# The output bias of the slot values: from row-of-ones products on TensorE to an addition on GpSimd

## The reference, cut to what matters

```python
x_in = _ln(ctx, lnkv_g, lnkv_b)              # 16 batches x 77 rows x 128
k = x_in @ wk + bk
v = x_in @ wv + bv
slots = q_mu + exp(q_logsig) * noise         # noise is the normalised x
for _ in range(3):
    prev = slots
    q = _ln(slots, lnq_g, lnq_b) @ wq + bq
    attn = softmax(k @ q.T / scale, over the slots) + 1e-8
    attn = attn / attn.sum(over the 77 rows)
    upd = attn.T @ v
    slots = upd @ wu + bu + prev
    h = _ln(slots, lnm_g, lnm_b) @ w1 + b1
    slots = gelu(h) @ w2 + b2 + slots
    slots = _ln(slots + x_cls, lnp_g, lnp_b)
```

## Time and profile before

| | |
|---|---|
| median of 3 runs | 912.81 us (910.27 to 913.75) |
| the profiled execution | 913.3 us, its span 911.5 us |
| TensorE matmul busy | 781.2 us, 86% |
| VectorE busy | 568.4 us, 62% |
| ScalarE busy | 529.7 us, 58% |
| GpSimd busy | 360.8 us, 40% |
| mean granted TensorE clock | 0.912 of full speed |

### The profile page before, as it was taken

How to read it: one execution, slowest core, us unless ns; L and a number is a source line. 1 busy time by engine, 2 the same in 40 slices (tenths; PEclk the granted TensorE clock), 3 DMA queues, 4 the chain that set the end, 5 groups by cost and what they waited for, 6 DMA issues and landing times.

```text
span 911.5 us, 18113 instructions
## 1 busy us (share of the span) xinstructions
PE 781.2 (86%) x5705; PEld 645.1 (71%) x5705; DVE 568.4 (62%) x1974; ACT 529.7 (58%) x1144; POOL 360.8 (40%) x561
## 2 busy tenths in 40 slices
PE   6988799999999999989988778999968786861693
PEld 5766678878888788777876547999646565651693
DVE  1667777787776667776767653333658787874012
ACT  3665566667666677656756422333359898841462
POOL 1233444343443333332346562665413232226363
PEclk9999899999999999999989979999757979785797
DMA  8324405340701520301140044886600000001574
GB/s 263 111 66 148 143 1 168 113 178 25 267 1 30 177 57 5 99 1 33 57 161 26 25 145 135 246 248 191 215 0 1 1 1 1 1 1 39 166 200 137
DMA packets 82057, 88.54 MB, mean 97 GB/s; under 512 B 6156, under 2 KB 69852, under 8 KB 81324
## 3 DMA queue, kind: packets, MB, share of 16 engines
q1 hardware_dynamic: 78475, 80.19, 29.1%
q0 software_dynamic: 3488, 7.20, 2.2%
HBM read 69.03 MB, written 35.17 MB: 114 GB/s over the span
## 4 chain that ended last, share of the span: by engine, by line
PE 58%; DVE 20%; issue 8%; ACT 6%; POOL 5%; DMA 1%; DVEq 0%; SPq 0%; POOLq 0%; ACTq 0%
PE bank L706 6%; PE bank L1017 6%; PE bank L700 6%; DVE sb_smax L1531 4%; PE bank L733 4%; PE bank L773 3%; DVE sb_row_sum L1540 3%; PE bank L742 3%; PE bank L1025 3%; PE bank L838 3%; PE bank L758 2%; PE bank L1126 2%; PE bank L1134 2%; PE bank L715 2%; DVE sb_st_all L1857 2%
## 5 line engine op out<-in xcount | busy, mean ns | idle before, releaser
L2035 POOL TENSOR_TENSOR sb_expd<-sb_expd,sb_rden 128x512 f32<-128x512 f32 (+1 forms) x128 | 112.4, 879 | 243.5 <-DVE sb_rden L1544 243.3
L1531 DVE TENSOR_REDUCE sb_smax<-bank 128x4 f32<-128x512 f32 (+1 forms) x128 | 74.0, 578 | 66.7 <-PE bank L733 35.6
L2127 POOL TENSOR_TENSOR sb_rstd_all<-sb_rsq_all,sb_halves 128x4 f32<-128x4 f32 x44 | 45.2, 1028 | 131.6 <-DVE sb_rsq_all L1864 131.6
L1254 ACT ACTIVATE sb_expd<-sb_shifted 128x512 f32<-128x512 f32 (+1 forms) x128 | 69.7, 544 | 43.4 <-DVE sb_shifted L1534 42.4
L1540 DVE TENSOR_REDUCE sb_row_sum<-sb_expd 128x4 f32<-128x512 f32 (+1 forms) x128 | 73.0, 570 | 8.4 <-ACT sb_expd L1254 8.4
L1534 DVE TENSOR_TENSOR sb_shifted<-bank,sb_smax 128x512 f32<-128x512 f32 (+1 forms) x128 | 74.9, 585 | 4.4
L700 PE MATMUL bank<-sb_h1T,sb_watt 128*128 128x128 f32 x512 | 71.3, 291 | 4.2 <-ACT sb_h1T L1153 2.3
L700 PEld LDWEIGHTS bank<-sb_h1T,sb_watt 128*128 128x128 f32 x512 | 65.5, 204 | 6.8 <-DMA sb_watt<-att_w 2.7
L1017 PE MATMUL bank<-sb_blk_xT,sb_up_w 128*128 128x128 f32 x456 | 57.1, 275 | 0.0
L1017 PEld LDWEIGHTS bank<-sb_blk_xT,sb_up_w 128*128 128x128 f32 x456 | 54.0, 192 | 0.0
L1824 DVE TENSOR_TENSOR sb_hid<-bank,sb_hid 128x384 f32<-128x384 f32 x38 | 21.2, 558 | 51.1 <-ACT sb_hid L1302 51.1
(11 more groups left out here) (270 smaller groups left out, 2006.9 us busy)
## 6 DMA issues: line engine op xcount, KB each, us to landing
sb_up_w<-gate_up SPq DMA_DIRECT2D x38, 384.0 KB
sb_v<-v_all SPq DMA_DIRECT2D x16, 576.0 KB, 6.6
rows_b<-pad_b SPq DMA_DIRECT2D x7, 1105.0 KB, 9.8
rows_a<-pad_a SPq DMA_DIRECT2D x7, 975.0 KB, 8.0
sb_up_w<-w1b SPq DMA_DIRECT2D x23, 256.0 KB
v_all<-sb_moe_w SPq DMA_DIRECT2D x14, 308.0 KB
sb_blk_x<-rows_a SPq DMA_DIRECT2D x38, 65.0 KB, 3.3
sb_picked<-back_a SPq DMA_DIRECT2D x4, 512.0 KB, 5.5
```

Of the source, the lines that this page charges most:

```text
L1254: act.activation(exp_of(i, s, j), shifted[:, u % 2, :, 0:n], ACT.Exp, scale=DH ** -0.5).then_inc(exp_done, 1)
L1531: dve.tensor_reduce(smax[:, u % 2, :], s_in, X, ALU.max).then_inc(max_done, 1)
L2035: pool.tensor_tensor(e, e, rden[:, u % 2, :].unsqueeze(2).broadcast_to([P, QH, n]), ALU.mult).then_inc(norm_done, 1)
```

## The change

The 16 row-of-ones products (32 MATMUL records) leave TensorE. `vu` is stored without the bias, and GpSimd adds it in place afterwards, with one TENSOR_TENSOR of 77 x 512 for each group, a new step "bias_u" in the order table. By the table's numbers GpSimd's order becomes: root_o(-1, 0), bias_u 0, bias_u 1, root_q(0, 0), root_o(-1, 1), root_q(0, 1), bias_u 2, root_o(-1, 2), root_q(0, 2), bias_u 3, root_m(0, 0). TensorE waits for `vu_ready` ahead of each of its 12 updates, besides the wait that it had.

```diff
 SLOT_STEPS = {
     (-1,): {
         "add": (-7.7126, -8.1139, -3.1663, -2.2100),
+        "bias_u": (-10.493, -11.492, -11.4, -11.7),
     },
...
+        vu_ready = sem("sl_vu_ready")
...
                 for n in range(4):
-                    pe.matmul(t[0:C, n * D:(n + 1) * D], ones[0:1, 0:C], R["bu"][0:1, :], start=True, stop=False)
-                    mm = pe.matmul(t[0:C, n * D:(n + 1) * D], vT[:, 4 * g + n, :], wus, start=False, stop=True)
+                    mm = pe.matmul(t[0:C, n * D:(n + 1) * D], vT[:, 4 * g + n, :], wus, start=True, stop=True)
                 mm.then_inc(pre_slot_full, 1)
...
                 if step == "update":
                     pe.wait_ge(att_ready, nth("shares", it, g))
+                    pe.wait_ge(vu_ready, nth("bias_u", -1, g))
...
-            for step, it, g in slot_steps("root_q", "root_m", "root_o", "send"):
+            for step, it, g in slot_steps("bias_u", "root_q", "root_m", "root_o", "send"):
+                if step == "bias_u":
+                    pool.wait_ge(pre_slot_done, 4 * G + 1 + g + 1)
+                    values = vu[:, 4 * g:4 * g + 4, 0:D]
+                    pool.tensor_tensor(values, values, R["bu"][0:C, :].unsqueeze(1).broadcast_to([C, 4, D]),
+                                       ALU.add).then_inc(vu_ready, 1)
```

## The result

The changed kernel takes 907.29 us (median of 4, 906.81 to 907.38), the one before 913.28 in the same comparison (median of 4, 910.27 to 914.61): ratio 0.9938, 95% interval 0.9919 to 0.9957. That is 6.0 us faster (3.9 to 7.4 by the interval); the forecast was 906.3. The profiled execution took 907.37 us, its span 905.6.

What follows compares the result with a forecast made beforehand. TensorE's alternating products were taken to bound the slot block (648.5 to 667.1 us), with VectorE late next; 9.8 - 1.75 - 0.75 - 0.5 - 0.3 = 6.5 us gave 906.3 us on the median's scale, own range 904 to 909, overall 901.5 to 911.

Steps and rivals of the forecast that it cites:

- The block gives 9.8 us: Slot block: with 16 products gone, VectorE is last and starts the first logits maximum at 663.6, 9.8 us earlier.
- the clock's fall would not matter to this: Slot block: whether the clock falls again at 651.2 does not change the 9.8 us, since VectorE is last either way.
- The block ends at 654.5 to 656.9: TensorE's slot block: the kept 16 products end at 656.9 (low clock) or 654.5 (high) instead of 667.1.
- Bias_u 0 and 1: GpSimd's first two additions hold back VectorE's second L1881 addition (0.95) and slots (0.8): 1.75 us lost, between 0 and 2.6.
- Bias_u 2: GpSimd's third addition holds back VectorE's two-input L1864 or L1870 near 663.3: 0.75 us lost, between 0 and 1.3.
- Bias_u 3: GpSimd's fourth addition races VectorE's nbias behind root_q(0, 2): 1.0 us lost if GpSimd wins, otherwise 0.1; taken as 0.5.
- The waits: TensorE's added wait before each of 12 updates, 0.1 us each, partly on the chain: 0.3 us lost, between 0 and 1.2.
- The sum: Whole kernel: 9.8 less 1.75, 0.75, 0.5 and 0.3 gives 6.5 us gained.
- let all that follows move by what the maximum moves: Everything behind the first logits maximum hangs on it, with no transfer due, and so moves earlier by the same amount.
- No holding back: Rival: VectorE and GpSimd don't disturb each other in this form; gain 9.5 us, 903.3; chance 0.15.
- The additions gain nothing on the path: Rival: the engines exclude each other whole and each wait costs 0.1; 6.1 us eaten, 3.7 stay, 909.1; chance 0.16.
- The clock cases: Rivals: clock rises early after 668, about 903, chance 0.12; or the rise near 696 is missed, 920, chance 0.07.

Runs made afterwards that it cites:

- e1: The changed kernel without the four GpSimd additions and without the new wait, so the output bias is left out: median 905.2 us.
- e3: The changed kernel with each GpSimd addition moved beside VectorE's one-input BATCH_NORM instructions, just before that group's root_q: 904.6 us.
- e4: The kernel before, with its one-row bias products replaced by 128-row products (identity and 128 copies of the bias row): 906.3 us, 6.9 faster than before.
- e6: The kernel before, with the 16 kept products also made one-row products (32 one-row, slot values left out); total time not given in the text.
- e5: The changed kernel with the wait for vu_ready only in the first iteration; total time not given, all twelve maxima within 0.1 us of the changed kernel's.

## Why the prediction was right

- *The block gives 9.8 us, since VectorE is last.* e1, e3 and e4: 9.9. That the clock's fall would not matter to this was not tested, since the clock stayed at 1.00 through the block in all three and in the changed kernel. In e6 it was low, but there 32 products kept TensorE until 656.8, 14.7 us after the first addition, and the first maximum came at 21.0.
- *The block ends at 654.5 to 656.9.* It ended at 652.8. The prediction took 0.37 us from the alternating products for the kept ones; alone they take 0.23. ScalarE then waited 6.5 us for VectorE, not 0.2, so the error cost nothing.
- *Bias_u 0 and 1: 1.75 us.* 0.86 + 0.66 = 1.5.
- *Bias_u 2: 0.75.* 0.7. The first maximum was 2.1 us later than in e1, the forecast had 2.5.
- *Bias_u 3: 0.5, as a race between 0.1 and 1.0.* GpSimd won: 0.9 (1.03 instead of 0.16).
- *The waits: 0.3.* Nothing that shows (e5, for eight of the 12). The row of a layer2 with 0.14 us was not evidence for a second wait's price.
- *The sum: 6.5.* 9.9 - 2.1 - 0.9 = 6.9 at the second maximum, and 6.8 at the last; 6.5 at the end of the span, 6.0 in the medians.
- *What was luck.* The terms missed in both directions and nearly cancel: 0.4 too much for the first three additions and 0.3 for the waits, 0.4 too little for the fourth. And the prediction let all that follows move by what the maximum moves. In the changed kernel it did, because the clock's rise came 6.9 us earlier as well (42.9 instead of 49.8 us after the first addition). Nothing in the prediction says why the rise should keep step, and in e3 and e4 it did not: of 9.9 us at the first maximum 7.2 to 7.3 were left at the last. With e3's 15.7 us between the third and fourth maximum, in place of 14.4, the gain here would have been about 1.4 us smaller (an estimate from these two traces).
- *The rivals.* "No holding back" is refuted by the durations in the changed kernel, and by e1 and e3, where they are gone and the maxima come earlier. "The additions gain nothing on the path": they ate 3.0 of the gain, not 6.1. The clock cases did not come, neither the early nor the missed rise. The Trainium skill's rule ("SBUF — State Buffer", section "SBUF: two separate sides"), that the shared port pair is held for a whole instruction also against VectorE instructions with two SBUF inputs, agrees: 0.86, 1.03 and the pairs above with an addition beside them, 0.87 unchanged for the one-input BATCH_NORM_STATS2.

## What to carry to other kernels

When a block is taken off the engine on the path, look at how long the next engine stands idle waiting for it: that, and not what the block loses, bounds the gain (9.9 us, where the block ended 14.9 us earlier). Work moved to GpSimd is not free where VectorE has just become last; put it beside VectorE instructions with one SBUF input: there the same four additions stretched nothing, and the first two maxima came as early as with no addition at all (e3). Before moving a bias product with a row of ones elsewhere, try it with as many rows as its neighbours.

## What was not expected of the hardware

- Products of one row and of 128 rows in turn cost 0.37 us each at the high clock and 0.64 at the low one. Products of 128 rows alone took 0.22 at the high clock (e4), those of one row alone 0.22 and 0.43 (e6).
- In a block of one-row products the clock fell from 1.00 to 0.50 with TensorE busy throughout (e6, within ten products); in one of as many products of 128 rows it stayed at 1.00 (e4, 7.2 us).
